# A decoder layer on one core: second tiles' block products first, last gates in their own buffer, last two phases reordered

## The reference, cut to what matters

```python
# attention: gated delta rule with two steps per token, H = 8 heads, 128 wide
q, k, v = l2norm/silu/conv4 of x @ Wq.T, x @ Wk.T, x @ Wv.T    # k and v have 256 steps, q 128
for each step: state = state * exp(g); v_new = (v - k @ state) * beta
               state = state + outer(k, v_new); o = q @ state
o = o * rsqrt(mean(o*o) + eps) * o_norm_w * silu(x @ Wg.T);  x = x + o @ Wo.T
x = x + wkv(t_decay, t_first, layernorm(x), ctx)              # scan over 128 tokens
x = x + moe(layernorm(x), gate_w, w1, w2, w3)                 # 12 experts, top 2, capacity
```

## Time and profile before

| what | us |
|---|---|
| median of three runs (lowest, highest) | 597.89 (597.41, 602.80) |
| the profiled execution: its own time | 599.72 |
| its span in the trace | 597.9 |
| busy: TensorE, VectorE, ScalarE | 552.3, 458.7, 365.6 |

### The profile page before, as it was taken

The page is one execution under the profiler, slowest core; times in us unless marked ns, Lnnn a source line. Parts: engine busy times, 40 slices in busy tenths (PEclk is TensorE's granted clock), DMA queues, the critical chain, the costliest instruction groups (busy, mean ns, idle before and its releaser), DMA issues.

```text
span 597.9 us, 15569 instructions
## 1 busy us (share of the span) xinstructions
PE 552.3 (92%) x6516; PEld 375.6 (63%) x6516; DVE 458.7 (77%) x1087; ACT 365.6 (61%) x651; POOL 40.7 (7%) x74
## 2 busy tenths in 40 slices
PE   8798889999999999999999999999998699767997
PEld 5446347576657666766676667667756688555646
DVE  5778888797888878887888788878794624799663
...
DMA packets 49702, 18.65 MB, mean 31 GB/s; under 512 B 39100, under 2 KB 48352, under 8 KB 49632
## 3 DMA queue, kind: packets, MB, share of 16 engines
...
## 4 chain that ended last, share of the span: by engine, by line
PE 73%; DVE 10%; ACT 9%; issue 3%; SPq 2%; DMA 1%; POOL 0%; DVEq 0%; ACTq 0%
PE bank L1439 17%; PE bank L1488 7%; DVE acc L979 5%; PE bank L1611 4%; PE bank L1607 4%; PE bank L1797 4%; PE bank L1491 3%; PE bank L1385 3%; PE bank L1569 3%; PE bank L1623 3%; PE bank L1617 2%; PE bank L1485 2%; PE bank L1619 2%; PE bank L1621 2%; PE bank L1859 2%
## 5 line engine op out<-in xcount | busy, mean ns | idle before, releaser
L979 DVE SCALAR_TENSOR_TENSOR acc<-bank,cw,acc 128x508 f32<-128x508 f32 (+2 forms) x240 | 176.5, 739 | 42.7 <-ACT acc L621 38.2
L1439 PE MATMUL bank<-xnT,wq 128*128 128x512 f32 x320 | 154.7, 610 | 12.4 <-DVE acc L979 11.5
L1439 PEld LDWEIGHTS bank<-xnT,wq 128*128 128x128 f32 x320 | 56.6, 191 | 72.1 <-issue 45.2
L621 ACT ACTIVATE acc<-bank,cw 128x512 f32<-128x512 f32 x80 | 55.4, 693 | 49.6 <-PE bank L1439 40.6
L1488 PE MATMUL bank<-kq 128*128 128x384 f32 x128 | 50.9, 497 | 0.0
L1012 DVE SCALAR_TENSOR_TENSOR AM<-bank,rb,DT 128x384 f32<-128x384 f32 x64 | 38.1, 607 | 1.8 <-PE bank L1488 1.5
L563 POOL TENSOR_TENSOR Yc<-T 128x256 f32<-128x256 f32 x7 | 4.3, 613 | 399.7 <-PE bank L1584 399.7
L638 ACT ACTIVATE vT<-acc 128x512 f32<-128x512 f32 x16 | 10.9, 679 | 33.3 <-DVE acc L979 33.2
L1078 DVE SCALAR_TENSOR_TENSOR xres<-bank,f,xres 128x256 f32<-128x256 f32 x56 | 23.7, 476 | 8.5 <-PE bank L1611 8.3
L1037 DVE TENSOR_TENSOR tmp<-Yl,Bl 128x15 f32<-128x15 f32 (+7 forms) x120 | 24.2, 201 | 6.9 <-DMA Bl<-blocks 4.8
L1491 PEld LDWEIGHTS bank<-kq 128*128 128x128 f32 x128 | 22.1, 190 | 10.4 <-issue 3.1
...
## 6 DMA issues: line engine op xcount, KB each, us to landing
...
blocks<-AM SPq DMA_DIRECT2D x128, 8.0 KB, 1.5
...
```

Source lines behind the costliest of these rows:

```text
L621: a(acc[:, u % RING, :, :], bank[6 + u % 2][:, :].rearrange("p (b l) -> p b l", b=4), ACT.Copy, scale=cw[:, t, 3:4]).then_inc(s_tap.next(f ...
L979: stt(w, ps[:, :, 0:L - s], cw[:, t, 3 - s:4 - s], w, ALU.mult, ALU.add).then_inc(s_cv.next(f"u{u}_{s}"), 1)
L1439: ins = mm(bank[6 + u % 2][:, :], wq[:, cc, t, :], xnT[:, cc, 512 * half:512 * half + 512], start=cc == 0, stop=cc == KC - 1)
```

## The change

- **Second tiles first.** In `PREP` and in all strings of TensorE and VectorE the four `e2` products come right behind `e1_1` and `e1_2`, and `e1_7` is the last of the twelve. `gather` takes the second tiles (c=1) first, behind `e2_3`, and the first tiles behind `e1_7`.
- **SyncE's last phase.** The gather comes before the load of head 7's gate weights, as in the other phases.
- **Last gates.** They go into `last_gate`, the first 128 columns of each batch of `DT1`. ScalarE waits for `e1_7` of head 7 instead of `o1'` of head 6.
- **Last two phases.** `vt0` to `vt3` and `yd` move from the end of NEXT to the start of LAST, `rq` ahead of the convolution's end. On VectorE all 30 `s` stand before `my0'`, with `vt2`, `ly'` and `vt3` between them. `ta0`, `ta1`, `tb0` come before `o1'`, and the joins of head 7 alternate with the rest of head 6. `on1` stands before `ms1`, and `n1` before `u0` (so `var2_1` comes before `U0` in POST_D).
- **Idle products.** 10, 6, 4, 6 and 3, again 29: ten instead of 13 ahead of `tb0`, six instead of three ahead of `lt0`.

The diff, without the strings of the first phase, which change in the same way as the middle ones:

```diff
@@ -62,7 +62,7 @@
 PREP = ([("dt0", "S"), ("dt1", "S"), ("dt2", "S"), ("cs", "S"), ("nrm", "V")]
-        + [(n, "V") for i in range(4) for n in (f"e1_{2 * i}", f"e1_{2 * i + 1}", f"e2_{i}")] + [(f"vt{i}", "V") for i in range(4)])
+        + [(n, "V") for n in "e1_0 e1_1 e2_0 e2_1 e1_2 e2_2 e2_3 e1_3 e1_4 e1_5 e1_6 e1_7".split()] + [(f"vt{i}", "V") for i in range(4)])
 SOLVE = ([("ga0", "S"), ("ga1", "S"), ("ta", "S"), ("tb", "V"), ("lt", "S"), ("ly", "V"), ("mt0", "S"), ("mt1", "S"), ("my0", "V"), ("my1", "V")]
@@ -79,39 +79,39 @@
                 "sq1' q1 rs' +7 cs +8 rt' -6 +9 -7 -8 ga0 ga1 -9 ta nr yd").split()
 VECTOR_ORDER = ("u u u u u u ly' u u u u s s u s s my0' my1' s s s s u s s s s u u u s s r2_0' s s r2_1' s s u u s s "
-                "u s s s s s s s s u s s u on0' u u u u on1' ms' u rb e1_0 rf' wo0' wo1' u e1_1 e2_0 e1_2 wo2' wo3' "
-                "xa u e1_3 u u u e2_1 e1_4 e1_5 e2_2 rq e1_6 tb xc e1_7 e2_3 vt0 vt1 vt2 vt3").split()
-
-TENSOR_ORDER = ("0 1 ly' 2 3 dt0 mt' dt1 4 my' dt2 w1_0' w1_1' r2_0' 5 r2_1' 6 w2_0' w2_1' o0' o1' 7 sa' rs' ca "
-                "cs 8 rn' nrm e1_0 e1_1 wo0' 9 e2_0 wo1' e1_2 wo2' wo3' ga0 e1_3 e2_1 e1_4 ga1 ta e1_5 e2_2 e1_6 tb "
-                "e1_7 e2_3 lt vt0 vt1 vt2 vt3").split()
+                "u s s s s s s s s u s s u on0' u u u u on1' ms' u rb e1_0 rf' wo0' wo1' u e1_1 e2_0 e2_1 wo2' wo3' "
+                "xa u e1_2 u u u e2_2 e2_3 e1_3 e1_4 rq e1_5 tb xc e1_6 e1_7 vt0 vt1 vt2 vt3").split()
+
+TENSOR_ORDER = ("0 1 ly' 2 3 dt0 mt' dt1 4 my' dt2 w1_0' w1_1' r2_0' 5 r2_1' 6 w2_0' w2_1' o0' o1' 7 sa' rs' ca cs 8 "
+                "rn' nrm e1_0 e1_1 wo0' 9 e2_0 wo1' e2_1 wo2' wo3' ga0 e1_2 e2_2 e2_3 ga1 ta e1_3 e1_4 e1_5 tb e1_6 "
+                "e1_7 lt vt0 vt1 vt2 vt3").split()
...
 NEXT_SCALAR_ORDER = ("lt' +0 -0 +1 +2 mt0' mt1' -1 w1_0' w1_1' +3 dt0 dt1 w2_0' +4 -2 w2_1' sq0' +5 -3 sq1' -4 rs' q0 +6 "
-                "-5 rt' q1 +7 dt2 cs +8 -6 -7 ga0 nr ga1 +9 -8 ta -9 yd").split()
-LAST_SCALAR_ORDER = ("lt' mt0' mt1' w1_0' w1_1' w2_0' w2_1' sq0' sq1' ga0 ta0 ga1 ta1 rs' yd0 lt0 lt1 xd0 yd1 mt0 xd1 rt' "
-                "mt1 w10 w11 w20 sq0 rs0 w21 rt0 sq1 rs1 dv0 rt1 x0 dv1 x1").split()
+                "-5 rt' q1 +7 dt2 cs +8 -6 -7 ga0 nr ga1 +9 -8 ta -9").split()
+LAST_SCALAR_ORDER = ("lt' yd' mt0' mt1' ga1 w1_0' w1_1' w2_0' ga0 sq0' ta0 w2_1' ta1 yd0 sq1' lt0 rs' xd0 xd1 lt1 mt0 yd1 "
+                "w10 mt1 rt' w20 w11 sq0 rs0 rt0 w21 sq1 rs1 dv0 rt1 x0 dv1 x1").split()
 NEXT_VECTOR_ORDER = ("u u u ly' u u s u s s u s s s u s my0' my1' s s s s s u s s s s s r2_0' s u u u s r2_1' s s s s s u "
-                "s u u on0' u s u on1' u ms' s s u rf' s wo0' wo1' u u u wo2' s wo3' u u rb e1_0 e1_1 e2_0 e1_2 e1_3 "
-                "e2_1 e1_4 e1_5 e2_2 e1_6 e1_7 u u xa e2_3 u u u u tb xc rq vt0 vt1 vt2 vt3").split()
-LAST_VECTOR_ORDER = ("s s s s s s ly' s s s s s s s s s s s s s s s s s s s my0' my1' s s s s s r2_0' r2_1' xa on0' on1' "
-                "tb0 xc0 tb1 xc1 ms' ly0 ly1 my0 my1 r20 rf' wo0' wo1' wo2' r21 on0 ms0 wo3' rf0 wa0 wb0 n0 ms1 on1 "
-                "rf1 m0 wa1 wb1 u0 n1").split()
-NEXT_TENSOR_ORDER = ("0 ly' 1 2 mt' dt0 dt1 my' 3 w1_0' w1_1' r2_0' r2_1' 4 w2_0' 5 w2_1' o0' o1' dt2 sa' rs' 6 rn' "
-                "wo0' ca wo1' 7 wo2' cs wo3' ga0 nrm e1_0 e1_1 8 e2_0 e1_2 e1_3 e2_1 e1_4 e1_5 e2_2 e1_6 e1_7 e2_3 "
-                "ga1 9 ta tb vt0 vt1 vt2 vt3").split()
-LAST_TENSOR_ORDER = ("lt' ga1 ly' ga0 mt' my' w1_0' w1_1' r2_0' r2_1' w2_0' w2_1' o0' o1' sa' ta0 ta1 rs' tb0 rn' "
-                "tb1 lt0 wo0' lt1 ly0 wo1' ly1 mt0 wo2' my0 mt1 w10 my1 r20 w11 w20 r21 o0 wo3' rs0 w21 rn0 wa0 wb0 "
-                "o1 rs1 rn1 wa1 wb1 E0 U0").split()
-
-IDLE = {"tb0": 13, "lt0": 3, "ly0": 4, "mt0": 6, "my0": 3}
+                "s u u on0' u s u on1' u ms' s s u rf' s wo0' wo1' u u u wo2' s wo3' u u rb e1_0 e1_1 e2_0 e2_1 e1_2 "
+                "e2_2 e2_3 e1_3 e1_4 e1_5 e1_6 e1_7 u u xa u u rq u u tb xc").split()
+LAST_VECTOR_ORDER = ("vt0 vt1 s s s s vt2 s s s s s s s s ly' vt3 s s s s s s s s s s s s s s s s s s my0' my1' r2_0' "
+                "r2_1' xa on0' tb0 xc0 on1' tb1 xc1 ly0 ly1 ms' my0 r20 my1 rf' wo0' wo1' wo2' on0 r21 wo3' ms0 rf0 "
+                "wa0 wb0 n0 on1 ms1 m0 rf1 wa1 wb1 n1 u0").split()
+NEXT_TENSOR_ORDER = ("0 ly' 1 2 mt' dt0 dt1 my' 3 w1_0' w1_1' r2_0' r2_1' 4 w2_0' 5 w2_1' o0' o1' dt2 sa' rs' 6 rn' wo0' "
+                "ca wo1' 7 wo2' cs wo3' ga0 nrm e1_0 e1_1 8 e2_0 e2_1 e1_2 e2_2 e2_3 e1_3 e1_4 e1_5 e1_6 e1_7 ga1 9 "
+                "ta tb").split()
+LAST_TENSOR_ORDER = ("vt0 vt1 lt' vt2 ly' vt3 ga1 mt' ga0 my' w1_0' w1_1' r2_0' r2_1' w2_0' w2_1' o0' ta0 ta1 tb0 o1' lt0 "
+                "sa' tb1 rs' ly0 rn' wo0' lt1 mt0 ly1 wo1' my0 mt1 w10 wo2' r20 my1 w20 w11 o0 wo3' r21 rs0 wa0 rn0 "
+                "w21 wb0 o1 rs1 rn1 wa1 wb1 E0 U0").split()
+
+IDLE = {"tb0": 10, "lt0": 6, "ly0": 4, "mt0": 6, "my0": 3}
 LAST = [("ga", "S"), ("ta", "S"), ("tb", "V"), ("lt", "S"), ("ly", "V"), ("mt", "S"), ("my", "V"), ("w1", "S"), ("r2", "V"), ("w2", "S"),
         ("o", "V"), ("rs", "S"), ("wa", "V"), ("wb", "V")]
@@ -246,6 +246,8 @@
         gate = sb("gate", [P, B, D])
+
+        last_gate = DT1[:, :, 0:D]
         sqO = R2
@@ -333,7 +335,7 @@
         s_yi = Signal(sem("solve_started_from_identity"), ["yi"], 16)
-        s_sc = Signal(sem("blocks_in_dram"), [f"{c}{q}" for c in range(2) for q in range(NB)], 16)
+        s_sc = Signal(sem("blocks_in_dram"), [f"{c}{q}" for c in (1, 0) for q in range(NB)], 16)
         s_bl = Signal(sem("blocks_gathered"), ["b"], 16)
@@ -367,7 +369,7 @@
         s_pa = Signal(sem("scalar_epilogue"), POST_A)
-        POST_D = (["var2_0", "nb2_0", "U0", "U1", "var2_1", "sB00", "sB01", "nb2_1", "sA00", "sA01", "U2", "U3", "den00", "den01", "num00", "num01", "sB10", "sB11", "den10", "den11"]
+        POST_D = (["var2_0", "nb2_0", "var2_1", "U0", "U1", "sB00", "sB01", "nb2_1", "sA00", "sA01", "U2", "U3", "den00", "den01", "num00", "num01", "sB10", "sB11", "den10", "den11"]
                   + [f"{n}0{cc}" for n in "piy" for cc in range(KC)] + ["sA10", "sA11", "x3_0", "x3_1", "var3_0",
@@ -412,13 +414,13 @@
                 AM = AMs[par][:, :, :].rearrange("p b (c n) -> p b c n", n=P)
-                for c, name in enumerate(("e1_7", "e2_3")):
+                for c, name in ((1, "e2_3"), (0, "e1_7")):
                     sp.wait_ge(prep.emptied(name).sem, prep.emptied(name).at(name, h))
...
                         sp.dma_start(dst, AM[r, :, 4 * c, r]).then_inc(s_sc.next(f"{c}{q}"), 16)
-                sp.wait_ge(s_sc.sem, s_sc.at(f"1{NB - 1}", h))
+                sp.wait_ge(s_sc.sem, s_sc.at(f"0{NB - 1}", h))
                 sp.dma_start(Bl[:, :, :], blocks[:, :, :]).then_inc(s_bl.next("b"), 16)
@@ -445,16 +447,12 @@
                 first, last = isinstance(h, int) and h == 0, isinstance(h, int) and h == H - 1
-                if last:
+                gather(h, par)
+                if not first:
                     sp.wait_ge(post.fills.sem, post.fills.at("ga1", h - 1))
-                    load_gate(h)
-                gather(h, par)
+                load_gate(h)
                 if last:
                     load_epilogue()
-                else:
-                    if not first:
-                        sp.wait_ge(post.fills.sem, post.fills.at("ga1", h - 1))
-                    load_gate(h)
                 scatter(h, not last)
@@ -733,18 +731,18 @@
                 if name == "ga":
-                    act.wait_ge(post.emptied("o1").sem, post.emptied("o1").at("o1", H - 2))
-                    a(gate[:, bs, :], four, ACT.Silu).then_inc(done, 1)
+                    act.wait_ge(prep.emptied("e1_7").sem, prep.emptied("e1_7").at("e1_7", H - 1))
+                    a(last_gate[:, bs, :], four, ACT.Silu).then_inc(done, 1)
                 elif name == "ta":
...
                 elif name == "yd":
-                    read(act, "my0")
                     act.wait_ge(ring.emptied("tb").sem, ring.emptied("tb").at("tb", H - 1))
...
                 elif name == "xd":
+                    read(act, "mt1")
                     act.wait_ge(s_lxc.sem, s_lxc.at(str(f)))
@@ -1149,7 +1147,7 @@
                 elif name == "ly":
-                    read(dve, "my0")
+                    read(dve, "mt1")
                     src = eight(ps, BLK)
@@ -1165,8 +1163,8 @@
                     dve.wait_ge(s_so2.sem, s_so2.at(str(f), h))
-                    stt(oTh[:, 512 * f:512 * f + 512], ring.tile("o")[:, :], onw[:, 0:1], gate[:, bs, :].rearrange("p b l -> p (b l)"),
-                        ALU.mult, ALU.mult).then_inc(ring.emptied("o").next("o"), 1)
+                    four_b = [t.rearrange("p (b l) -> p b l", b=4) for t in (oTh[:, 512 * f:512 * f + 512], ring.tile("o")[:, :])]
+                    stt(four_b[0], four_b[1], onw[:, 0:1], last_gate[:, bs, :], ALU.mult, ALU.mult).then_inc(ring.emptied("o").next("o"), 1)
                 elif name == "ms":
@@ -1210,6 +1208,8 @@
```

(12 more changed lines are left out.)

2 lines of the change are left out of this document (removed).

## The result

The changed kernel took 595.64 us (median of 19 runs, 592.55 to 599.07), the kernel before 598.66 beside it (19 runs, 595.93 to 603.40): ratio 0.9945, interval 0.9922 to 0.9968. So 3.0 us were won where 7.0 were forecast. The changed kernel's profiled execution took 594.45 us, span 592.7; before it was 597.9, so this pair of profiles shows 5.2.

The account below looks back on a forecast made before the run. TensorE bounds the middle phases and joins, SyncE's gather-to-`xa` chain the last phase between. Joins start 7.4 us earlier, minus 1.5 within them, plus 1.1 at the end: 597.9 - 7.0 = 590.9 us, range 588 to 594.5.

Parts of the forecast that it names:

- Step 1: Middle phases: swapped orders use the same slots and nothing waited for the gathered blocks; 0, within 0.2 us either way.
- Step 2: Gather of head 7: issued earlier, so the substitution's first multiply comes at 456.2 instead of 462.33, 6.1 us earlier.
- Step 3: Substitution of head 7: 10.6 us with its insertions instead of 11.15, ending at 466.8, 6.7 us earlier; `ly'` doesn't wait.
- Step 4: Way through DRAM to `xa`: 7.8 us plus 1.0 for loads ahead of `solved` (bounds 0, 1.1); `xa` 5.7 earlier.
- Step 5: Head 6 beside the substitution: full clock expected, `o0'` ends at 474.9, joins start at 476.4 instead of 483.8, 7.4 earlier.
- My own case for the lower clock: Head 6's work ahead of the joins: at the lower clock `o0'` would end at 477.4 instead of 474.9.
- Step 6: Joins of head 7: 33.0 us TensorE work plus 1.0 idle (bounds 0, 4.5); `o1` ends at 510.4, 5.9 earlier.
- rival (a): The new order waits for itself: blocks at 457.8, idle of the joins grows to 4.5 us; 596.0 us, chance 0.20.
- Rival (c): Clock falls in the wait for `Yc`; one low stretch costs 5.2 us, two give 602.3, slower than before; chance 0.05.
- Step 7: End of head 7, `o1` to `wa1`: `on1` first readies VectorE's factors 1.1 us sooner (bounds 0 and 1.6).
- Step 8: Epilogue: 0, only earlier; bounds 2 us less or 3 us more, depending on where the lower clock falls.
- the forecast's own range: Whole kernel: 588 to 594.5 us, from late blocks (1.6), head 6's clock (1.1) and bounds of steps 4, 7 and 8.

Follow-up runs that it names:

- after: The changed kernel, nothing edited, first series and its profile: 595.64 us, ratio 0.9945 to the kernel before; profiled span 592.7.
- after_again: The changed kernel once more, nothing edited, with a profile: 593.74 us, ratio 0.9903 to the kernel before; profiled span 590.9.
- before: The kernel before, nothing edited, its first profile: profiled execution 599.72 us, span 597.9.
- before_look: The kernel before, nothing edited, profiled a second time: 601.38 us.
- after_third: The changed kernel a third time, nothing edited, on a third chip: 595.01 us, ratio 0.9901 to the kernel before.
- after_look: The changed kernel, nothing edited, profiled a fourth time: 596.84 us.

## Why the prediction was right and wrong

**Step 1, right** as far as the profiles can tell. The second-last phase's `rb` came at 436.34 us in `after`, before at 436.55. Over the changed kernel's four it lies between 435.49 and 437.34, over the two of the kernel before at 436.55 and 437.89.

**Step 2, right.** First multiply 456.36, 454.96, 456.46, 456.71 in the four profiles, forecast 456.2.

**Step 3, a wait left out.** The substitution with its insertions took 11.8 to 12.0 us in all four profiles for 10.6. The difference is the wait ahead of `vt2`, 1.31 to 1.50 us: TensorE does `vt2` behind `lt'`, and both ran at the lower clock. At the full clock `lt'` took 0.8 less (above) and eight `vt` instructions 1.09 us in `after_again`, where four took 1.11 at the lower one; by an estimate from these rows that is 1.3 of the 1.47 in `after`. I had looked only at the wait that `ly'` might bring. The substitution ended at 468.3 to 468.7 for 466.8, and at 466.8 only in `after_again`, where it had begun 1.2 us early.

**Step 4, the size right on average, the bounds too narrow.** From the last subtract's end to `xa` I had 7.8 us and 1.0 more. The four profiles have 7.75, 9.94, 9.45 and 9.09, so between nothing and 2.2 more. From `solved` to `Yc` it took 2.52, 3.91, 3.55 and 2.56 us for 1.75. The loads were also issued later than I thought (461.96, 460.41, 462.10, 462.31 for 459.6), as `vt3` was later. With the loads behind the store the issues took 1.75 again, and the whole way 7.1. So the rule that I drew from the Trainium skill, DMA: Bandwidth & Descriptors, section Queues, rings and completion order, agrees with these runs, and its price can be twice what I let it cost.

**Step 5, the place right, the clock wrong: here the prediction failed first.** "So I expect the full clock" held only from 463.3 to 465.1 on and not from 459: the low stretch had begun at 451.4 to 453.4, inside or behind a gap that both kernels have within `tb` (1.79 us, 1.52 before), and lay on `lt'`, `vt` and `ga1` for 10.2 to 13.6 us in all four profiles. In `after` `my1'` ended at 470.83 for 468.2, 1.5 of it from the substitution and 1.10 as a wait for TensorE, which `ga1` had held 1.55 us longer; `o0'` ended 7.0 us behind it (I had 6.7), and `ta0` started at 477.72. My own case for the lower clock had 477.4. In the other three `xa` ended last, at 477.4, 478.6 and 478.5 for 476.3, as the substitution had ended late (in two) and the way through DRAM took longer. The joins began 1.2 to 2.4 us later than forecast, 1.8 on average, 5.1 to 6.3 earlier than before.

**Step 6, the work right, the clock put at nothing.** Without a fall the joins took 32.9 to 33.0 us where I had 34.0: TensorE's idle time in them was 0.9, not the 4.5 of rival (a). The measured 595.64 lies next to that rival's 596.0, but the idle joins of that rival did not occur; what did is a wait of the new order elsewhere, ahead of `vt2`. All 33.0 us were priced at the full clock, and that held in only two of four profiles. Rival (c) named the mechanism, with one stretch of 10.3 us or two, and only as a way to end slower. The stretches are 3.4 and 6.8 us and take back 1.4 and 3.1 of the gain. As a loss that comes in part of the executions it belonged in the sum and in the likeliest case. On average over the four the joins cost 1.7 us more than before, where I had 1.5: the term was met by two errors that cancel.

**Step 7, right** (1.3 for 1.1) except where the low stretch covers the last output products: 12.6 us in `after`, so nothing was won there in that execution.

**Step 8, right.** *Rest* is 69.4 us in 15 of the 20 profiles and 69.5 in two. The other three have a low stretch between 551 and 561 us, right ahead of the experts or in them, and take 0.8, 1.7 and 3.4 more: my upper bound was 3. The upper bounds that I named for the forecast's own range add up to 6.9 us (597.8), not to its 594.5, which takes them as not coming together; I did not say so.

**The sum.** Profile by profile, against the 597.9 of `before` (against `before_look` each would show 1.7 more):

```
after        first 6.0  ta0 6.2   joins -0.6        tail -0.3   = 5.2
after_again  first 7.4  ta0 6.3   joins -0.6        tail +1.3   = 7.0
after_third  first 5.9  ta0 5.1   joins -2.0 (1.4)  tail +1.3   = 4.4
after_look   first 5.6  ta0 5.2   joins -3.7 (3.1)  tail +1.3   = 2.8
```

(`ta0`, joins and tail add up, to 0.1; `first` is contained in `ta0`; in brackets the clock's part.) The mean of the four is 4.9. Of the 2.1 us that it lacks 1.7 are missing at `ta0` (steps 3 to 5), 0.2 in the joins and 0.2 in the tail. From one execution to the next it is the joins that differ most, by 3.2 us. So the term that failed is the time at the lower clock, which the forecast put at nothing: in the substitution and ahead of the joins in every profile, in the joins in two of four.

What separates 3.0 in the first series from 6.0 and 5.0 in the later two lies in both kernels: the median of the kernel before was 598.66 for 599.72 and 600.01, that of the changed one 595.64 for 593.74 and 595.01. For the changed kernel it can be the clock: an execution had 38.3 us at the lower clock in the first (mean of 19), 33.2 in the second and 34.9 in the third, and over the executions of one kernel the span rises by some 0.3 us for each (0.2 to 0.3 in these three series), which gives 1.5 and 1.0 for its 1.9 and 0.6. Why the kernel before was faster in the first series, and why a stretch falls into the joins of one execution and not of the next, stays open: I have moved, filled and reordered the waits ahead of them, and no run settled what starts it.
